# TensorE's order in the second layer: expert down products six to nine and the next group's row turning stand among other up products

## The chip, the cores and the metric

The kernel runs on one core of one Trainium2 chip. The metric is the device time of one execution in microseconds (us), as the median of several runs. In the trace the engines are called PE (TensorE, matrix products), PEld (its weight loads), DVE (VectorE), ACT (ScalarE), POOL (GpSimd) and SP (SyncE, which only issues transfers here).

## What is computed

The input is 32 sequences of 256 tokens with 128 channels. Two layers follow each other, each of the form x = x + s * g. The first has an RWKV-like branch and a small binarised feed-forward branch; the change does not touch it. The second is, cut to what matters:

```python
xn = layernorm(x)
# branch s: a selective scan
xr = xn @ W_in;  x_in, res = halves of xr
xc = silu(causal depthwise conv of 4 taps over x_in + conv_b)
p  = xc @ W_x
delta = softplus(p[:, :16] @ W_dt + b_dt);  B = p[:, 16:32];  C = p[:, 32:]
h  = h * delta + B * xc            # over time, 16 states
s  = (h.sum(states) * C * silu(res)) @ W_out
# branch g: 2 shared and 16 routed experts of width 64
shared = gelu(xn @ shared_up) @ shared_down
gate   = softmax(xn @ router), only the best 4 of 16 kept
routed = (gelu(xn @ routed_up) * gate) @ routed_down
x = x + s * silu(shared + routed)
```

## The kernel before

The 8192 tokens are cut into 16 groups (`G`) of 512. All channels lie on the 128 partitions, so one matrix product has 128 x 512 results and fills one of the eight banks of PSUM. Every engine has its own instruction list, written out by hand in program order, and the lists are tied by semaphores (`wait_ge` before an instruction, `then_inc` behind it). An engine never runs past a wait; what stands behind it in its list waits too.

The second layer is a pipeline over groups. In body n every engine works on group f = n (the front of the work: products with `W_in`, convolution, router, the experts' up products and gelus), group m = n - 1 (the scan, the experts' down products) and group t = n - 2 (the final product and sum). There are 18 bodies; in bodies 1 to 15 both f and m exist. `paired` peels the first three and the last three bodies and loops over the rest in pairs.

The experts are handled in nine pieces (`UC` = 9) of 128 rows: piece 0 holds the two shared experts, pieces 1 to 8 the routed ones. For each piece c:

- `expert_in(c)` on PE is the up product of group f: three half-precision matmuls with `upH`, `upH`, `upL` into `q_U[(c + 1) % 2]`. There are only two such banks, so for c of 2 and more it waits on `b_act` until gelu c - 2 has read its bank.
- `gelu(c)` on ACT (L613) reads that bank and writes `act[:, c, :]`.
- The gate multiplies pieces 1 to 8: POOL does pieces 1 to 3 (`GP` = 3, L443), DVE pieces 4 to 8 (`gated`, L938, which counts `b_actg`).
- `expert_out(c)` on PE is the down product of group m: one fp32 matmul with `dnT` (recorded as two passes) that adds piece c into the bank `q_F`. Its inputs were made in the body before (gelu) and by POOL or DVE.

Two more pieces of PE work stand among the up products. `turn_rows(q_D[1])` (L1069) turns the normalised rows of group f + 1 with four 128 x 128 matmuls against the identity; it waits on `b_xn` (the rows are there) and `b_cr` (DVE's `output_weight(1)`, L960, has read the bank). `gates_turned` (L1241) turns the gates of group f. ACT's `turned_high` (L537) reads the turned rows behind its gelu 5, and DVE's `turned_low` (L884) later.

Behind the last up product PE runs the final product of group m with `w_out` (it waits on `b_y`, DVE's L986), and then the next body: `low_rank` (`s1W`), `conv_in` (`w_inH`), the router, `residual_in`, `steps` (`s2W`, waits on `b_zl`, which DVE's `low_z` L943 counts), `turn_back`, `expert_out(0)` and `(1)`, `output_weights` (`wcH`, `wcL`), `s2B`, `expert_out(2)` to `(4)`, then up product 0.

ACT's list of a body, in order: `ffn_silu` (L555), `high_z` (L575), `conv_input` (L562), `step_size` (L580) and `res_silu` (L569) in turn, `conv_silu` (L588, twice), a table load (L632), exponentials and logarithms (L592, L639, L602, L596), a table load (L644), gelu 0 and 1, `high_xc(1)`, gelu 2 to 5, `turned_high`, gelu 6 to 8, `gates_out` (L550), a table load (L654).

DVE's list, in order: `row_stats` (L673), the product `sg` (L996, needs ACT's L555), `low_z` (L943, needs ACT's L575), the router's maximum (L1004, needs the router product of PE), moments, L1010, the six convolution taps (L926), the normalised rows (L891), gated pieces and `output_weight` (L960), the choice of four (L901 to L917), L1033, `scan_input` (L969), two gated pieces (L938), L953, the scans (L979), `output` (L986), `low_xc` (L965), `turned_low` (L884).

Of the kernel before, what the change touches and what calls it, by code (L numbers as in the profile page):

```python
# [39 lines left out]
def build(nc, A, out):  # L40
# [16 lines left out]
    UC = (NS + NR) * E // P  # L57
# [13 lines left out]
    with ExitStack() as ctx:  # L71
# [187 lines left out]

        b_T, b_K, b_V, b_RX, b_Z0, b_Z1, b_S, b_F = bank  # L260
        q_T, q_Q, _, _, _, _, q_S, q_F = bank
        q_D = (bank[2], bank[3])
        q_U = (bank[4], bank[5])
# [5 lines left out]
        def after(eng, semaphore, value):  # L269

            if not (isinstance(value, int) and value <= 0):
                eng.wait_ge(semaphore, value)

        def has(n):

            return not isinstance(n, int) or 0 <= n < G
# [779 lines left out]
        def _(pe):  # L1056
            def mm(ps, lhsT, rhs, start=True, stop=True):
                return nc.tensor.matmul(ps, lhsT, rhs, start=start, stop=stop)  # L1058

            def split3(ps, wh, wl, h, l):  # L1060

                mm(ps, wh, h, True, False)
                mm(ps, wh, l, False, False)
                return mm(ps, wl, h, False, True)

            def turn_rows(ps):

                for j in range(J):
                    last = nc.tensor.transpose(ps[:, j::J], xn[:, j, :], ident[:, :])  # L1069
                return last  # L1070
# [99 lines left out]
            def xc_product(ps, wh, wl, i):  # L1170
# [5 lines left out]
                    last = mm(ps[:, :], wl[:, k, w], xch[:, k, :], False, k == IC - 1)  # L1176
                return last

            def layer1(n, par):
                f, m, t = n, n - 1, n - 2  # L1180
                XH, XL = (xh, xh_)[par], (xl, xl_)[par]
# [33 lines left out]
                def expert_in(c):  # L1215
                    if c >= 2:
                        pe.wait_ge(sem["b_act"], UC * f + c - 1)
                    else:
                        pe.wait_ge(sem["b_conv"], IC * f * (TAPS - 1) + CONV_DONE[1 - c])
                    w = slice(c * P, (c + 1) * P)  # L1220
                    split3(q_U[(c + 1) % 2][:, :], upH[:, w], upL[:, w], XH[:, :], XL[:, :]).then_inc(sem["b_up"], 1)

                def expert_out(c):

                    if c > GP:
                        pe.wait_ge(sem["b_actg"], GV * m + c - GP)
                    elif c:
                        pe.wait_ge(sem["b_actp"], GP * m + c)
                    else:
                        pe.wait_ge(sem["b_act"], UC * m + 1)  # L1230
                        after(pe, sem["b_g"], m)
                    h = prod[:, c - 1, :] if c else act[:, 0, :]
                    mm(q_F[:, :], dnT[:, c * P:(c + 1) * P], h, c == 0, c == UC - 1).then_inc(sem["b_down"], 1)

                def gates_turned():
                    pe.wait_ge(sem["b_gx"], f + 1)
                    pe.wait_ge(sem["b_lg"], f + 1)
                    if has(t):
                        pe.wait_ge(sem["b_out"], t + 1)
                    for j in range(J):  # L1240
                        last = nc.tensor.transpose(q_Q[:, j::J], gx[:, j, :, :].rearrange("p r i -> p (r i)"), ident[:, :])  # L1241
                    last.then_inc(sem["b_gtT"], 1)
# [31 lines left out]
                if has(m):  # L1274
# [9 lines left out]
                    expert_out(2)  # L1284
                    expert_out(3)
                    expert_out(4)
                if has(f):
                    expert_in(0)
                    expert_in(1)
                for c in range(2, UC):  # L1290
                    if has(f):
                        expert_in(c)
                    if has(m) and c >= 5:
                        expert_out(c)
                    if has(f) and c == 5:
                        gates_turned()
                    if has(f) and has(f + 1) and c == 4:
                        pe.wait_ge(sem["b_xn"], f + 2)
                        after(pe, sem["b_cr"], IC * (m + 1))
                        turn_rows(q_D[1]).then_inc(sem["b_xnT"], 1)  # L1300
# [9 lines left out]
            pe.wait_ge(sem["prep_out"], NB)  # L1310
            pe.wait_ge(sem["prep_sbuf"], 1)
            paired(pe, layer1)


# [25 lines left out]
```

## Time and profile before

| | |
|---|---|
| time, median of 3 runs | 738.07 us (735.55 to 738.98) |
| the profiled execution's own time | 734.49 us |
| its span in the trace | 732.7 us |
| busy PE / DVE / ACT / POOL | 642.5 / 635.7 / 509.4 / 281.5 us |
| mean granted clock of TensorE | 0.976 of full |
| gelu 0 of body 1, of body 15 | at 334.54 us, at 697.31 us |

Busy time is the time in which an engine had an instruction under way; it is no proof that the engine was the limit. Times in the trace run from the span's start. The first layer and the preparation of weights fill the span up to about 300 us; the second layer fills the rest.

### The profile page before, as it was taken

What the parts mean: (1) busy time and instruction counts of PE and PEld (TensorE: products, weight loads), DVE (VectorE), ACT (ScalarE), POOL (GpSimd) and SP (SyncE); (2) the same over time, 40 slices, a digit from 0 to 9 for tenths busy, and PEclk for the clock granted to TensorE, in tenths of its full rate; (3) what the DMA queues carried; (4) which work ended last, traced back from release to release, by engine and by line L of the source; (5) the groups of instructions that cost most, each with busy time, mean ns of one, the idle gap of its engine ahead of it and who ended that gap; (6) DMA issues with size and microseconds to landing.
All of it is one profiled execution on the core that took longest, in us unless ns stands there. A gap on an engine that the chain in (4) does not pass through costs nothing. (4 is left out here: it accounts for less than half of the span.)

```text
span 732.7 us, 10841 instructions
## 1 busy us (share of the span) xinstructions
PE 642.5 (88%) x2711; PEld 304.7 (42%) x2711; DVE 635.7 (87%) x1467; ACT 509.4 (70%) x800; POOL 281.5 (38%) x278
## 2 busy tenths in 40 slices
PE   2795899999999985598999899999999999999986
PEld 1342444444444442343444444444444444544432
DVE  4996999999999997758988988988898898889766
ACT  2463566766666652687877887787788779788775
POOL 6456666777767762031222123032212303221220
PEclk9898999999999997899999999999999999999999
DMA  5420000000000000000000000000000000000000
GB/s 151 110 90 26 0 0 0 0 0 0 0 0 0 1 0 1 0 1 0 15 1 15 15 0 14 14 14 0 14 14 0 14 14 14 0 14 14 1 16 29
DMA packets 10739, 11.29 MB, mean 15 GB/s; under 512 B 4800, under 2 KB 6288, under 8 KB 10720
## 3 DMA queue, kind: packets, MB, share of 16 engines
q1 hardware_dynamic: 9744, 10.73, 4.8%
q0 software_dynamic: 112, 0.33, 0.2%
q8 instruction: 8, 0.13, 0.1%
q10 hardware_dynamic: 864, 0.00, 0.1%
q14 instruction: 11, 0.09, 0.0%
HBM read 6.87 MB, written 4.19 MB: 15 GB/s over the span
## 5 line engine op out<-in xcount | busy, mean ns | idle before, releaser
L1058 PE MATMUL bank<-arena,w 128*128 128x512 f16 x640 | 153.9, 389 | 20.0 <-DVE arena L717 14.1
L1058 PE MATMUL bank<-arena,dnT 128*128 128x512 f32 x288 | 138.6, 592 | 0.0
L613 ACT ACTIVATE arena<-bank,xinv 128x512 f32<-128x512 f32 x144 | 95.6, 687 | 51.0 <-PE bank L1058 50.8
L443 POOL TENSOR_TENSOR arena<-arena 128x512 f32<-128x512 f32 x48 | 59.7, 1271 | 151.8 <-ACT arena L550 151.8
L1058 PEld LDWEIGHTS bank<-arena,w 128*128 128x128 f16 x640 | 63.4, 100 | 99.0 <-issue 24.5
L476 ACT ACTIVATE arena<-bank 128x512 f16<-128x512 f32 x96 | 53.9, 606 | 35.1 <-PE bank L1058 35.1
L433 POOL TENSOR_TENSOR arena<-arena 128x512 f32<-128x512 f32 x16 | 17.1, 1067 | 150.5 <-DVE arena L917 150.5
L1058 PE MATMUL bank<-arena,wsqT 128*128 128x512 f32 x128 | 65.6, 617 | 6.0 <-DVE arena L726 6.0
L1058 PEld LDWEIGHTS bank<-arena,dnT 128*128 128x128 f32 x288 | 53.7, 191 | 36.0 <-issue 24.3
L926 DVE SCALAR_TENSOR_TENSOR arena<-bank,cws,arena 128x506 f32<-128x506 f32 (+1 forms) x96 | 67.1, 740 | 1.1
L717 DVE SCALAR_TENSOR_TENSOR arena<-bank,arena 128x512 f16<-128x512 f32 x96 | 60.2, 670 | 1.7 <-ACT arena L476 0.5
L938 DVE TENSOR_TENSOR arena<-arena 128x512 f32<-128x512 f32 x80 | 52.1, 684 | 0.0
L396 POOL TENSOR_TENSOR arena<-arena 128x512 f16<-128x512 f32 x32 | 36.9, 1155 | 30.3 <-ACT arena L476 22.9
L1058 PE MATMUL bank<-xh,upH 128*128 128x512 f16 x72 | 28.1, 391 | 19.4 <-ACT arena L613 15.6
L473 ACT ACTIVATE arena<-bank 128x512 f32<-128x512 f32 x32 | 19.1, 597 | 32.9 <-PE bank L1058 32.9
L996 DVE TENSOR_TENSOR sg<-bank,gp 128x512 f32<-128x512 f32 x16 | 11.1, 691 | 34.4 <-ACT gp L555 32.3
L1058 PE MATMUL bank<-xh_,upH 128*128 128x512 f16 x72 | 28.1, 390 | 14.5 <-ACT arena L613 14.5
L400 POOL TENSOR_TENSOR arena<-arena 128x512 f32<-128x512 f32 x16 | 20.3, 1269 | 51.0 <-DVE arena L753 51.0
L979 DVE TENSOR_TENSOR_SCAN arena<-arena 128x256 f32<-128x256 f32 x64 | 38.9, 669 | 0.0
L1058 PE MATMUL bank<-arena,wcH 128*128 128x512 f16 x128 | 38.1, 379 | 0.0
L1058 PEld LDWEIGHTS bank<-arena,wsqT 128*128 128x128 f32 x128 | 25.4, 200 | 22.9 <-issue 9.6
L1058 PE MATMUL bank<-arena,w_out 128*128 128x512 f32 x64 | 30.2, 594 | 3.1 <-DVE arena L986 3.1
(208 smaller groups left out, 1525.3 us busy)
## 6 DMA issues: line engine op xcount, KB each, us to landing
x_all<-in_L_attn_x SPq DMA_DIRECT2D x16, 256.0 KB, 2.7
out<-x_all SPq DMA_DIRECT2D x16, 256.0 KB, 2.0
up_n<-in_L_ffn_routed_up SPq DMA_DIRECT2D x1, 512.0 KB, 3.8
dn_n<-in_L_ffn_routed_down SPq DMA_DIRECT2D x1, 512.0 KB, 5.4
wx<-in_L_attn_W_x SPq DMA_DIRECT2D x1, 288.0 KB, 2.8
k_u<-in_L_ffn_k POOLq DMA_DIRECT2D x1, 256.0 KB, 5.1
w_in<-in_L_attn_W_in SPq DMA_DIRECT2D x1, 256.0 KB, 2.4
k_u<-in_L_ffn_k SPq DMA_DIRECT2D x1, 128.0 KB, 5.7
```

The lines of the kernel that those rows point to most:

```text
L396: g.tensor_tensor(hl[:, 1, j, :], relu[:, j, :], hh[:, 1, j, :], ALU.subtract).then_inc(sem["a_low"], 1)
L400: g.tensor_tensor(ya[:, :], ysr[:, :], rec[:, :], ALU.mult).then_inc(sem["a_y"], 1)
L433: g.tensor_tensor(gx[:, :, :, :], gt[:, :, :].unsqueeze(3).to_broadcast(wide), rs[:, :].unsqueeze(2).unsqueeze(3).to_broadcast(wide), ALU. ...
L443: g.tensor_tensor(prod[:, c, :], act[:, c + 1, :], gate[:, :], ALU.mult).then_inc(sem["b_actp"], 1)
L473: a.activation(relu[:, j, :], src, ACT.Relu).then_inc(sem["a_relu"], 1)
L476: a.activation(hh[:, layer, j, :], src, ACT.Relu).then_inc(sem[("a_hi0", "a_hi1")[layer]], 1)
L613: a.activation(act[:, c, :], q_U[(c + 1) % 2][:, :], ACT.Gelu, scale=xinv[:, I_UP:I_UP + 1]).then_inc(sem["b_act"], 1)
L717: v.scalar_tensor_tensor(hl[:, layer, j, :], b_Z[layer][j][:, :], 0.0, hh[:, layer, j, :], ALU.max, ALU.subtract).then_inc(sem[("a_lo0", " ...
L926: v.scalar_tensor_tensor(uk, seqs(q_U[k][:, :])[:, :, 0:T - back], cws[:, k, t:t + 1], uk, ALU.mult, ALU.add)\
L938: v.tensor_tensor(prod[:, c, :], act[:, c + 1, :], gate[:, :], ALU.mult).then_inc(sem["b_actg"], 1)
L979: last = v.tensor_tensor_scan(H[:, k, w], delta[:, k, w], bx[:, k, w], 0.0, ALU.mult, ALU.add)
L1058: return nc.tensor.matmul(ps, lhsT, rhs, start=start, stop=stop)
```

## The change

The table `DOWN_BEHIND` says behind which up product of group f a down product of group m stands. Before, down product c (5 to 8) stood behind up product c, and the row turning behind up product 4. After, down products 5, 6, 7 and 8 stand behind up products 1, 3, 6 and 7, and the row turning stands behind up product 1, after down product 5. `gates_turned` stays behind up product 5. Waits and increments of each moved piece go with it unchanged; nothing is added or removed.

```diff
+            DOWN_BEHIND = {1: 5, 3: 6, 6: 7, 7: 8}
+
...
-                if has(f):
-                    expert_in(0)
-                    expert_in(1)
-                for c in range(2, UC):
+                for c in range(UC):
                     if has(f):
                         expert_in(c)
-                    if has(m) and c >= 5:
-                        expert_out(c)
+                    if has(m) and c in DOWN_BEHIND:
+                        expert_out(DOWN_BEHIND[c])
                     if has(f) and c == 5:
                         gates_turned()
-                    if has(f) and has(f + 1) and c == 4:
+                    if has(f) and has(f + 1) and c == 1:
                         pe.wait_ge(sem["b_xn"], f + 2)
                         after(pe, sem["b_cr"], IC * (m + 1))
                         turn_rows(q_D[1]).then_inc(sem["b_xnT"], 1)
```

The lists of ACT, DVE and POOL stay as they are. PE's list in body 2 of the kernel before, from the last matmul of up product 1 to the row turning (`upH` and `upL` are up products of three matmuls each, `dnT` a down product, `ident,xn` the row turning):

```order
L1058 MATMUL bank<-xh,upL 128x512
L1058 MATMUL bank<-xh,upH 128x512
L1058 MATMUL bank<-xl,upH 128x512
L1058 MATMUL bank<-xh,upL 128x512
L1058 MATMUL bank<-xh,upH 128x512
L1058 MATMUL bank<-xl,upH 128x512
L1058 MATMUL bank<-xh,upL 128x512
```

The same place in the changed kernel, from the last matmul of up product 1 to down product 6:

```order
L1058 MATMUL bank<-xh,upL 128x512
L1058 MATMUL bank<-arena,dnT 128x512
L1069 MATMUL bank<-ident,xn 128x128 x4
L1058 MATMUL bank<-xh,upH 128x512
L1058 MATMUL bank<-xl,upH 128x512
L1058 MATMUL bank<-xh,upL 128x512
L1058 MATMUL bank<-xh,upH 128x512
L1058 MATMUL bank<-xl,upH 128x512
L1058 MATMUL bank<-xh,upL 128x512
L1058 MATMUL bank<-arena,dnT 128x512
```

One down product and the row turning now stand between up products 1 and 2, and another down product between 3 and 4, where up products followed each other directly.

The end of the same body on PE before, from up product 7 to the final product (`w_out`):

```order
L1058 MATMUL bank<-xh,upH 128x512
L1058 MATMUL bank<-xl,upH 128x512
L1058 MATMUL bank<-xh,upL 128x512
L1058 MATMUL bank<-arena,dnT 128x512
L1058 MATMUL bank<-xh,upH 128x512
L1058 MATMUL bank<-xl,upH 128x512
L1058 MATMUL bank<-xh,upL 128x512
L1058 MATMUL bank<-arena,dnT 128x512
L1058 MATMUL bank<-arena,w_out 128x512 x2
```

And in the changed kernel:

```order
L1058 MATMUL bank<-xh,upH 128x512
L1058 MATMUL bank<-xl,upH 128x512
L1058 MATMUL bank<-xh,upL 128x512
L1058 MATMUL bank<-arena,dnT 128x512
L1058 MATMUL bank<-xh,upH 128x512
L1058 MATMUL bank<-xl,upH 128x512
L1058 MATMUL bank<-xh,upL 128x512
L1058 MATMUL bank<-arena,w_out 128x512 x2
```

The last up product is now directly followed by the final product; no down product stands between them.

## Rows read from the trace of the kernel before

**Rows 1.** Stretch; busy PE, PEld, DVE, ACT, POOL (instructions); granted clock; DMA share; GB/s.
```profile
335.00:340.00 5.00, 4.72 (x16) 2.17 (x17) 5.00 (x9) 3.47 (x6) 0.83 (x1) 0.66 0.00 0
350.00:700.00 350.00, 325.14 (x1407) 155.09 (x1406) 312.05 (x826) 283.56 (x424) 78.96 (x80) 1.00 0.03 11
```

**Rows 2.** Who waited for whom, 350 to 720 us: total us, times, longest.
```profile
ACT arena L613 <- PE bank L1058: 45.0, 69, 1.3
...
DVE sg L996 <- ACT gp L555: 28.7, 14, 3.3
PE bank L1058 <- ACT arena L613: 24.9, 28, 1.6
```

**Rows 3.** PE in order of time, one body: start, us, what, [idle before <-releaser].
```profile
541.47 0.38 PE L1058 MATMUL bank<-xh_,upL 128*128 128x512 f16 x1
543.34 0.39 PE L1058 MATMUL bank<-xh_,upH 128*128 128x512 f16 x1 [1.50 <-ACT arena L613]
...
545.10 0.39 PE L1058 MATMUL bank<-xh_,upH 128*128 128x512 f16 x1 [0.30 <-ACT arena L613]
...
545.76 0.60 PE L1069 MATMUL bank<-ident,xn 128*128 128x128 f32 x4
...
546.85 1.02 PE L1058 MATMUL bank<-arena,dnT 128*128 128x512 f32 x2
...
552.66 1.88 PE L1058 MATMUL bank<-arena,w_out 128*128 128x512 f32 x4
554.38 1.03 PE L1058 MATMUL bank<-arena,s1W 128*128 128x512 f16 x4
...
557.58 0.59 PE L1058 MATMUL bank<-arena,s2W 128*128 128x512 f16 x2
```

**Rows 4.** ACT in order of time, the same body and the start of the next.
```profile
542.60 1.27 ACT L613 ACTIVATE arena<-bank,xinv 128x512 f32<-128x512 f32 x2
...
552.08 0.69 ACT L613 ACTIVATE arena<-bank,xinv 128x512 f32<-128x512 f32 x1 [0.82 <-PE bank L1058]
...
555.44 0.60 ACT L575 ACTIVATE arena<-bank 128x512 f16<-128x512 f32 x1 [0.28 <-PE bank L1058]
...
562.14 0.63 ACT L588 ACTIVATE arena<-arena 128x512 f32<-128x512 f32 x1 [0.81 <-DVE arena L926]
...
568.44 1.26 ACT L613 ACTIVATE arena<-bank,xinv 128x512 f32<-128x512 f32 x2
```

**Rows 5.** DVE in order of time, the same stretch.
```profile
549.36 1.26 DVE L986 TENSOR_TENSOR arena<-arena 128x512 f32<-128x512 f32 x2
...
551.87 0.68 DVE L884 SCALAR_TENSOR_TENSOR xl<-bank,xh 128x512 f16<-128x512 f32 x1
...
555.20 0.69 DVE L996 TENSOR_TENSOR sg<-bank,gp 128x512 f32<-128x512 f32 x1 [1.87 <-ACT gp L555]
556.07 0.68 DVE L943 SCALAR_TENSOR_TENSOR arena<-bank,arena 32x512 f16<-32x512 f32 x1 [0.18 <-ACT arena L575]
557.18 0.23 DVE L1004 TENSOR_REDUCE arena<-bank 128x4 f32<-128x64 f32 x1 [0.43 <-PE bank L1058]
...
557.84 4.26 DVE L926 SCALAR_TENSOR_TENSOR arena<-bank,cws,arena 128x506 f32<-128x506 f32 x6
...
566.18 0.74 DVE L960 SCALAR_TENSOR_TENSOR arena<-bank,fac,arena 128x512 f32<-128x512 f32 x1
```

**Rows 6.** ACT, gelu 0 of body 1, gelus 0 and 8 of body 15.
```profile
334.54 1.27 ACT L613 ACTIVATE arena<-bank,xinv 128x512 f32<-128x512 f32 x2
...
697.31 1.26 ACT L613 ACTIVATE arena<-bank,xinv 128x512 f32<-128x512 f32 x2
...
706.28 0.69 ACT L613 ACTIVATE arena<-bank,xinv 128x512 f32<-128x512 f32 x1 [0.82 <-PE bank L1058]
```

**Rows 7.** PE in body 0: up product 2, and the row turning.
```profile
312.23 0.61 PE L1058 MATMUL bank<-xh,upH 128*128 128x512 f16 x1 [2.93 <-ACT arena L613]
...
315.49 0.60 PE L1069 MATMUL bank<-ident,xn 128*128 128x128 f32 x4
```

## The prediction

> **What bounds the kernel now.** I read the stretches first, then the waits, then one body in order of time on PE, ACT and DVE. Between 350 and 700 us PE is busy for 325.14 of 350 us, DVE for 312.05 and ACT for 283.56 [rows 1]. No engine is full, so the period of a body is set by a loop over several engines. The waits name it: in 14 bodies PE waited 28 times for ACT's gelus, 24.9 us in all, ACT's gelus waited 69 times for PE, 45.0 us, and DVE's `sg` waited 14 times for ACT's L555, 28.7 us [rows 2].
>
> One period runs from gelu 0 at 542.60 to gelu 0 at 568.44, 25.84 us [rows 4]. Bodies 1 to 15 are 362.77 us apart over 14 periods [rows 6], 25.91 on average, so this period is typical. Its chain has five links. (a) Gelu 0 to gelu 8, 542.60 to 552.08: 9.48 us, in which ACT waits for PE (0.82 before gelu 8) [rows 4]. (b) Gelu 8 to `sg` on DVE at 555.20, through `gates_out`, a table load and L555: 3.12 us [rows 4, 5]. (c) `sg` to the first convolution tap at 557.84: 2.64 us, with three waits in or beside it: 0.28 of ACT's `high_z` for PE's `low_rank` [rows 4], 0.18 of DVE's `low_z` for `high_z`, and 0.43 of L1004 for PE's router product [rows 5]. (d) The taps, until they release ACT's second `conv_silu` at 562.14: 4.30 us. (e) ACT alone, to the next gelu 0: 6.30 us [rows 4]. The sum is 25.84.
>
> PE has holes. Up product 1's last matmul starts at 541.47 and up product 2 starts at 543.34, when gelu 0 has freed the bank. The three matmuls of an up product take 0.66 us from start to start (545.10 to the turning at 545.76), so one takes 0.22 and this hole is 1.65 us. Up products 2 and 3 end at 544.64 (543.34 + 2 x 0.65), and up product 4 starts at 545.10: a hole of 0.46. Together that is 2.11 us in a period; PE has work for the other 23.73 [rows 3].
>
> **Sizes of the moved pieces** [rows 3]. From the turning at 545.76 to down product 5 at 546.85 are 1.09 us; less an up product of 0.65 that leaves 0.44 for the turning (`gates_turned`, also four small matmuls, is put at 0.44 too). From 546.85 to `w_out` at 552.66 are 5.81 us: four down products, one `gates_turned`, three up products. (5.81 - 0.44 - 3 x 0.65) / 4 = 0.86 us for a down product.
>
> **The change, in the clock of this body.** Down product 5 and the turning (0.86 + 0.44 = 1.30) move into the first hole. They must not be late: DVE works in list order, and its second L960 is behind everything that they need (the gated piece, the normalised rows, the freed bank). It ends at 566.92, in this body's terms 25.84 earlier, at 541.08, before PE is there at 541.69 [rows 5]. So up product 2 still starts at 543.34. Up product 3 ends at 544.64, down product 6 fills the second hole and more, to 545.50, and from there PE is paced by nothing: from 543.34 on there are seven up products, `gates_turned` and three down products, 4.55 + 0.44 + 2.58 = 7.57, which ends at 550.91 instead of 552.66. PE's `w_out` comes 1.75 us earlier. It needs DVE's L986, done at 549.36 + 1.26 = 550.62 [rows 5]: 0.3 to spare. The following `w_inH` then stands at 550.91 + 1.72 + 0.86 = 553.49 and needs L884, done at 552.55 [rows 3, 5].
>
> Link (a): up product 8 is now last, with no down product behind it, so it starts 0.65 before 550.91, at 550.26; before, it started at 552.66 - 0.86 - 0.65 = 551.15, and gelu 8 followed 0.93 later. Gelu 8 moves from 552.08 to 551.19, **0.89 less**. Earlier gelus cover it: gelu 4 gets 0.4 later by down product 6, but the bank for up product 6 is free in time by a few hundredths.
>
> Link (b) is unchanged, `sg` at 554.31. Link (c): ACT could start `high_z` at 555.16 - 0.89 = 554.27, and PE's `low_rank`, 1.75 earlier, is done (555.44 - 1.75 = 553.69). So that 0.28 goes; `low_z` follows `sg` without its 0.18. L1004's 0.43 goes as well, since PE's router product is 1.75 earlier and DVE less than that. **0.61 to 0.7 less**, depending on how tightly DVE's instructions follow each other; I take 0.7, since rows that follow directly on DVE start some 0.05 to 0.1 before the end shown of the last (557.84 + 4.26 = 562.10 against 562.14 shows the other end of that spread). Links (d) and (e) hold no wait for PE. A period so loses 0.89 + 0.7 = **1.6 us**, to 24.24. PE's own check: its `steps` would start at 557.58 - 1.75 = 555.83, `low_z` ends about 555.6; and of the 2.11 us of holes 0.5 remain, before up product 2. Both loops close.
>
> **The sum.** 14 periods x 1.6 = 22.4. Body 15 has no turning: gelu 8 stands 8.97 after gelu 0 [rows 6], and would stand 8.59 after it, 0.4 less, and nothing in the tail needs the old order. In body 0 there are no down products, but the turning, which stood in a stretch that PE paced, moves into a wait of 2.93 us [rows 7]: 0.4. Together 23.2 us. The profiled execution took 734.49, so it would take 711.3. The median of the runs before is 738.07, 3.6 above the profiled one; 738.07 - 23.2 gives **714.9**. A difference within 0.5% (3.7 us) can't be told from none here.
>
> **Bounds of the unknown.** No row shows two pieces in the hole or the tightened hand-over of link (c). From above, PE's whole idle time is the most that can go in a period: 2.11 x 14 + 0.8 = 30.3. To that comes the clock of body 1 (below), at most 1.0: 738.07 - 31.3 = 706.8. From below, only gelu 8 moves and link (c) gives nothing: 0.89 x 14 + 0.8 = 13.3, so 724.8. I stay near the middle term since the three waits of link (c) are each in a row with PE or ACT as what ended them.
>
> **The rivals.**
>
> *Only link (a) shrinks.* What would hold link (c): DVE's list between `sg` and the taps finds another late partner, such as ACT's `conv_input` behind `high_z`, or PE's `w_out`, with only 0.3 to spare, waits for L986 and takes the rest of PE with it. Against it: a PE 0.3 later still has 0.5 of hole left. 724.8 us; chance 0.1.
>
> *More than forecast.* From 335 to 340 us, body 1, the granted clock is 0.66, so PE was for part of it at its lower level of 1.2 GHz instead of 2.4, behind the longest hole of that body; from 350 to 700 it is 1.00 [rows 1]. The 14 periods hold 362.77 - 14 x 25.84 = 1.0 us beyond the typical period [rows 6], the most that this lower clock can have cost. With the hole filled by 1.30 us of work the clock may stay up. Then 713.9, and with PE's holes gone too the 706.8 above; chance 0.05 for something below 711. The Trainium skill (TensorE: Matmul & The Clock Gate, "A second HAM failure mode: psum-queue depth-cycling") says that PE's short idle times between groups of matmuls can make the clock swing between its levels. By that rule every body's clock would gain from filled holes; the trace does not agree: with 2.11 us of holes in each period the clock is 1.00 over 350 us.
>
> *Slower.* The moved pieces carry their waits in front of up product 2. If the turning had to wait for DVE (`b_cr`, L960), up product 2 and all gelus would be queued behind it. Now L960 is done at 541.08, while PE is free for the turning at 542.55 and needs it done by 543.34, thus started by 542.90. The period gets longer than now only where L960 comes more than 541.08 -> 542.90 + 1.6, 3.4 us later against gelu 0. Against it: L960 and gelu 0 both follow the taps, through DVE and ACT, so nothing pulls them apart. With 4 us late in each of 14 periods it would be 0.6 x 14 = 8 us slower, 746; chance 0.03. The Trainium skill (same page, "Step-by-step: what each phase is for") states that only weight loads are pulled ahead and matmuls keep program order, which is why one late wait here would hold the ups; no run here shows it yet.
>
> *The change does nothing.* If the period were set by a loop that PE's order doesn't touch, filled holes would only reappear elsewhere. DVE is the candidate: but it idles 1.87 + 0.18 + 0.43 = 2.48 us a period, for ACT and PE [rows 5]. 738; chance 0.04.
>
> **How the numbers follow.** Forecast 0.78, only link (a) 0.1, more 0.05, none 0.04, slower 0.03. The forecast's own range is 711 to 719 (1.35 to 1.8 us a period, and the spread of the runs); with link (a) alone and the clock taken in, 709 to 723 leaves out no more than 2 in 10. Faster by over 0.5%: 0.78 + 0.1 + 0.05 = 0.93; same 0.04; slower 0.03.
>
> **What the profile after would show.** The hole before up product 2 at about 0.5 and none before up product 4; gelu 0 to gelu 8 in 8.6 us; DVE's waits before L943 and L1004 gone and the one before `sg` near 1 us; gelu 0 to gelu 0 in 24.2 us; body 1 to body 15 in 340. The prediction is wrong if `w_out` or `steps` shows a wait for DVE, or if the turning shows one for L960.

## The result

The changed kernel takes 713.89 us (median of 4 runs, 711.37 to 714.81); the kernel before took 738.04 in the same comparison (735.55 to 738.98). The ratio is 0.9694, with a 95% interval of 0.9668 to 0.972, so the gain is between 20.7 and 24.5 us. The forecast was 714.9 us, a gain of 23.2.

In the stretches (busy time of PE, PEld, DVE, ACT, POOL with instruction counts, then the granted clock), the changed kernel's PE is busy for 341.87 of 350 us, against 325.14 before [rows 1]. The first stretch lies ahead of body 1 and is taken up further down:

```profile
300.00:305.00 5.00, 4.22 (x23) 1.67 (x22) 2.33 (x14) 1.55 (x2) 0.05 (x1) 0.52 0.00 0
340.00:690.00 350.00, 341.87 (x1483) 164.34 (x1481) 326.67 (x853) 292.57 (x443) 84.35 (x84) 1.00 0.03 11
```

The waits of the changed kernel from 340 to 700 us (total us, times, longest) answer to [rows 2]. PE waits for gelus 14 times instead of 28 and for 7.5 us instead of 24.9; one of its two holes (stretches in which it idles) in each body is gone.

```profile
DVE sg L996 <- ACT gp L555: 17.8, 15, 2.8
...
PE bank L1058 <- ACT arena L613: 7.5, 14, 0.7
```

One body of the changed kernel on PE, to be held against [rows 3]:

```profile
530.61 0.38 PE L1058 MATMUL bank<-xh_,upL 128*128 128x512 f16 x1
530.83 1.02 PE L1058 MATMUL bank<-arena,dnT 128*128 128x512 f32 x2
531.69 0.60 PE L1069 MATMUL bank<-ident,xn 128*128 128x128 f32 x4
532.84 0.39 PE L1058 MATMUL bank<-xh_,upH 128*128 128x512 f16 x1 [0.56 <-ACT arena L613]
...
534.15 1.02 PE L1058 MATMUL bank<-arena,dnT 128*128 128x512 f32 x2
535.01 0.38 PE L1058 MATMUL bank<-xh_,upH 128*128 128x512 f16 x1
...
540.40 1.88 PE L1058 MATMUL bank<-arena,w_out 128*128 128x512 f32 x4
...
545.32 0.59 PE L1058 MATMUL bank<-arena,s2W 128*128 128x512 f16 x2
```

Down product 5 and the turning start without a wait right behind up product 1, down product 6 leads to up product 4 without one, and `w_out` and `steps` (`s2W`) wait for nothing; the L986 that `w_out` needs ends at 540.14, 0.26 ahead of it. The same body on ACT:

```profile
532.10 1.26 ACT L613 ACTIVATE arena<-bank,xinv 128x512 f32<-128x512 f32 x2
...
540.68 0.69 ACT L613 ACTIVATE arena<-bank,xinv 128x512 f32<-128x512 f32 x1 [0.82 <-PE bank L1058]
...
543.66 0.59 ACT L575 ACTIVATE arena<-bank 128x512 f16<-128x512 f32 x1
...
550.19 0.63 ACT L588 ACTIVATE arena<-arena 128x512 f32<-128x512 f32 x1 [0.81 <-DVE arena L926]
...
556.48 1.27 ACT L613 ACTIVATE arena<-bank,xinv 128x512 f32<-128x512 f32 x2
```

And on DVE:

```profile
538.87 1.27 DVE L986 TENSOR_TENSOR arena<-arena 128x512 f32<-128x512 f32 x2
...
543.79 0.69 DVE L996 TENSOR_TENSOR sg<-bank,gp 128x512 f32<-128x512 f32 x1 [0.95 <-ACT gp L555]
544.52 0.68 DVE L943 SCALAR_TENSOR_TENSOR arena<-bank,arena 32x512 f16<-32x512 f32 x1
545.23 0.23 DVE L1004 TENSOR_REDUCE arena<-bank 128x4 f32<-128x64 f32 x1
...
545.89 4.26 DVE L926 SCALAR_TENSOR_TENSOR arena<-bank,cws,arena 128x506 f32<-128x506 f32 x6
```

`high_z` (L575), `low_z` (L943) and L1004 had waits of 0.28, 0.18 and 0.43 before [rows 4, 5] and have none now. The period shown is 24.38; over the 12 periods from body 2 to body 14 it is 24.42 on average (the table loads L644 before gelu 0 stand at 359.86 and 652.91), against 25.85 before. The periods alternate between 24.38 or 24.39 and 24.46 or 24.47, because gelu 8 to `sg` takes 3.11 in one body and 3.20 in the next (565.06 to 568.26):

```profile
565.06 0.69 ACT L613 ACTIVATE arena<-bank,xinv 128x512 f32<-128x512 f32 x1 [0.82 <-PE bank L1058]
...
568.26 0.69 DVE L996 TENSOR_TENSOR sg<-bank,gp 128x512 f32<-128x512 f32 x1 [1.03 <-ACT gp L555]
```

The kernel before has the same 0.09 between its bodies, but there the wait for PE's router product took it up, and from body 4 to body 14 its periods lie between 25.83 and 25.85.

### The profile page after: what moved, and what is told of

Same layout as the page of the kernel before. It is cut to its first block and busy times, and to the rows that moved or that the text cites. A ratio compares the mean times of both kernels' runs of the same rounds, so it can differ in the third digit from the quotient of the medians.

```text
span 713.0 us, 10841 instructions
## 1 busy us (share of the span) xinstructions
PE 643.3 (90%) x2711; PEld 306.4 (43%) x2711; DVE 636.2 (89%) x1467; ACT 504.4 (71%) x800; POOL 281.5 (39%) x278
## 5 line engine op out<-in xcount | busy, mean ns | idle before, releaser
L588 ACT ACTIVATE arena<-arena 128x512 f32<-128x512 f32 x32 | 20.2, 631 | 20.3 <-DVE arena L926 20.3
```

Of the source, the lines that this page charges most:

```text
L588: a.activation(xc[:, par, k, :], u[:, k, :], ACT.Silu).then_inc(sem["b_xc"], 1)
```

## The experiments

The theory under test is that of the prediction, here called the loop theory: a period is gelu 0 to gelu 8, paced by the PE work between up products 2 and 8, plus the hand-over from `sg` to the taps, in which PE's `low_rank` and router product end waits only while they are late. The main rival is that PE's filled holes are all that counts. The edits below change two things in the changed kernel: the table (written with tuples, so that several down products can stand behind one up product) and the place of the turning. Times of different comparisons are set against each other by their ratios to the kernel before.

**Down product 5 alone in the hole**

```diff
-            DOWN_BEHIND = {1: 5, 3: 6, 6: 7, 7: 8}
+            DOWN_BEHIND = {1: (5,), 6: (6,), 7: (7,), 8: (8,)}
...
-                    if has(f) and has(f + 1) and c == 1:
+                    if has(f) and has(f + 1) and c == 4:
```

> The order of before, except that down product 5 stands behind up product 1 (6, 7 and 8 behind their own up products, the turning behind up product 4). Loop theory (the period is gelu 0 to gelu 8 paced by PE, plus the hand-over from sg to the taps): 0.86 us of PE work leaves the stretch between up products 2 and 8, the hole before up product 4 stays, PE and ACT both come 0.86 earlier, so high_z still waits 0.28 for PE and the hand-over gives nothing. A period 0.86 shorter, 14 x 0.86 + 0.9 = 12.9 us, about 725. Rival A (the gain comes from the end of the body, where no down product stands behind the last up product): nothing, 738. Rival B (the turning, which frees ACT's turned_high early, carries the gain): nothing, 738.

Measured: 723.12 us, ratio 0.9839 (0.9798 to 0.988); period 24.99. `high_z` still waits for PE, as this row of ACT shows:

```profile
522.68 0.60 ACT L575 ACTIVATE arena<-bank 128x512 f16<-128x512 f32 x1 [0.27 <-PE bank L1058]
```

The period is 0.86 shorter, one down product, as expected. The ratio is a gain of 1.6%, 11.7 us of 734.78, where 12.9 was expected. Both rivals gave this kernel nothing; neither can be the only source of the gain.

**The turning alone**

```diff
-            DOWN_BEHIND = {1: 5, 3: 6, 6: 7, 7: 8}
+            DOWN_BEHIND = {5: (5,), 6: (6,), 7: (7,), 8: (8,)}
```

> The order of before, except that the row turning stands behind up product 1. Loop theory: 0.44 us leaves the paced stretch, 14 x 0.44 + 0.4 = 6.6 us less, about 731.5. Rival A: nothing, 738. Rival B: most of the measured gain, about 715 to 720.

Measured: 728.82 us, ratio 0.991 (0.9876 to 0.9945); period 25.41, 0.44 shorter, as expected. The turning alone is less than a third of the 1.43 us that the change takes out of a period, so rival B falls.

**Both of them**

```diff
-            DOWN_BEHIND = {1: 5, 3: 6, 6: 7, 7: 8}
+            DOWN_BEHIND = {1: (5,), 6: (6,), 7: (7,), 8: (8,)}
```

> Both of these moves, down products 6, 7 and 8 as before. Loop theory: the two add up, 1.30 us a period, the hole before up product 4 stays at 0.46, high_z still waits 0.28 for PE: 14 x 1.30 + 1.3 = 19.5 us less, about 718.5. Rival A: 738, all of the change's gain is missing. If the two don't add up, both pieces compete for one hole of which less than 1.30 counts.

Measured: 717.6 us, ratio 0.9767 (0.9724 to 0.9809); period 24.55, 1.30 shorter. The two add up, and rival A, which gave this kernel nothing, falls. So the other moves of the change (6 behind 3, 7 behind 6, 8 behind 7) are worth only 24.55 - 24.42 = 0.13 us a period together. The next run takes them apart.

**Down product 8 behind the last up product again**

```diff
-            DOWN_BEHIND = {1: 5, 3: 6, 6: 7, 7: 8}
+            DOWN_BEHIND = {1: (5,), 3: (6,), 6: (7,), 8: (8,)}
```

> The changed kernel, except that down product 8 stands behind up product 8 again instead of behind up product 7. PE does the same work in the same holes. Loop theory: gelu 8 comes 0.86 earlier than in the changed kernel (7.7 us after gelu 0 instead of 8.6), so that PE's router product and low_rank end the hand-over again; both are 1.76 earlier than in the kernel before, so a period is 24.08 instead of 24.4: 14 x 0.33 = 4.6 us faster than the changed kernel, about 709.5. Rival C (PE alone sets the pace, and the filled holes are all that counts): as the changed kernel, 714. Rival A: slower than the changed kernel by up to 12 us, 720 to 726.

Measured: 708.37 us, ratio 0.9647 (0.9607 to 0.9687); period 24.08, as worked out. The interval of the ratio overlaps that of the changed kernel (0.9668 to 0.972); it is the periods of the traces, from body 2 to 14 24.07 or 24.08 in all but one case here and 24.38 to 24.47 there, that tell the two apart. On ACT, gelus 7 and 8 start at 533.41 and follow each other, `high_z` waits for PE once more, and the next gelu 0 is at 550.42; PE's `w_out` is at 534.64:

```profile
526.34 1.27 ACT L613 ACTIVATE arena<-bank,xinv 128x512 f32<-128x512 f32 x2
...
533.41 1.33 ACT L613 ACTIVATE arena<-bank,xinv 128x512 f32<-128x512 f32 x2 [0.82 <-PE bank L1058]
...
537.42 0.60 ACT L575 ACTIVATE arena<-bank 128x512 f16<-128x512 f32 x1 [0.27 <-PE bank L1058]
...
550.42 1.27 ACT L613 ACTIVATE arena<-bank,xinv 128x512 f32<-128x512 f32 x2
```

```profile
534.64 1.88 PE L1058 MATMUL bank<-arena,w_out 128*128 128x512 f32 x4
```

PE does the same work in the same holes as in the changed kernel, `w_out` stands 8.30 us after gelu 0 in both (540.40 - 532.10 and 534.64 - 526.34), and yet a period is 0.34 shorter. The rival that only filled holes count falls: it gives these two the same time. In the changed kernel PE had become earlier than ACT and DVE could use. Down product 6 behind up product 3 and 7 behind 6 are worth 24.55 - 24.08 = 0.47 a period, and 8 behind 7 costs 0.34 of it.

**Down products 7 and 8 behind the last up product**

```diff
-            DOWN_BEHIND = {1: 5, 3: 6, 6: 7, 7: 8}
+            DOWN_BEHIND = {1: (5,), 3: (6,), 8: (7, 8)}
```

> The changed kernel, except that down products 7 and 8 both stand behind up product 8. Loop theory, with the hand-over bound by PE as in e4 (there gelu 0 followed w_out by 15.78 us): gelu 8 comes another 0.4 earlier, at 7.3 us, but up product 8 must wait 0.4 for gelu 6 and w_out slips to 8.7 us after gelu 0. Period 8.7 + 15.8 = 24.5, as the changed kernel's 24.4 or 0.1 worse: 714 to 716 on the scale of 738 for before, ratio 0.970 to 0.973. Rival D (the sooner gelu 8, the better): another 0.4 less than e4, ratio 0.957.

Measured: 714.25 us, ratio 0.9716 (0.9675 to 0.9756); period 24.46, where 24.5 was worked out. PE's up product 8 waits for gelu 6, and `w_out` comes 515.14 - 506.46 = 8.68 us after gelu 0; ACT's `high_z` then waits 1.13 us for PE:

```profile
512.77 0.39 PE L1058 MATMUL bank<-xh,upH 128*128 128x512 f16 x1 [0.21 <-ACT arena L613]
...
515.14 1.88 PE L1058 MATMUL bank<-arena,w_out 128*128 128x512 f32 x4
```

```profile
506.46 1.27 ACT L613 ACTIVATE arena<-bank,xinv 128x512 f32<-128x512 f32 x2
...
513.71 0.69 ACT L613 ACTIVATE arena<-bank,xinv 128x512 f32<-128x512 f32 x1 [0.34 <-PE bank L1058]
...
517.92 0.60 ACT L575 ACTIVATE arena<-bank 128x512 f16<-128x512 f32 x1 [1.13 <-PE bank L1058]
```

In this kernel as in the last one the next gelu 0 follows `w_out` by 15.78 us (550.42 - 534.64, and 515.14 + 15.78 = 530.92, where the trace has it), and the kernel before has the same 15.78 (568.44 - 552.66) [rows 3, 4]. Gelu 8 stands 513.71 - 506.46 = 7.25 us after gelu 0, sooner than in any other kernel here, and the period is still longer than in the last one: rival D falls. A sooner gelu 8 is worth nothing once PE is the later partner of the hand-over.

**A down product whose input is late in the hole: the rival that ended slower**

```diff
-            DOWN_BEHIND = {1: 5, 3: 6, 6: 7, 7: 8}
+            DOWN_BEHIND = {1: (7,), 3: (5,), 6: (6,), 7: (8,)}
```

> The changed kernel with the down products permuted so that number 7 stands behind up product 1 (then 5 behind 3, 6 behind 6, 8 behind 7). Its input is DVE's third piece from the end, done 2.65 us after gelu 0, so PE must wait in front of the turning and of up product 2. This is the rival that ended slower: up product 2 starts 2.70 + 0.86 + 0.44 = 4.0 us after gelu 0 instead of 0.74, gelu 8 at 11.8, period 11.8 + 15.8 = 27.6, 1.8 more than before: 14 x 1.8 + 2 = 27 us slower than before, ratio 1.037. If TensorE's clock falls in the hole of over 3 us, up to 1.7 us more in each body, ratio up to 1.07. If matmuls could pass the waiting one, nothing of this and about 0.97.

Measured: 801.65 us, ratio 1.0887 (1.0839 to 1.0934); period 30.69. PE in one body, whose gelu 0 is at 546.84, the gated pieces 7 and 8 on DVE, and the stretches behind the hole:

```profile
549.58 2.07 PE L1058 MATMUL bank<-arena,dnT 128*128 128x512 f32 x2 [3.81 <-DVE arena L938]
551.45 1.06 PE L1069 MATMUL bank<-ident,xn 128*128 128x128 f32 x4
552.30 0.63 PE L1058 MATMUL bank<-xh,upH 128*128 128x512 f16 x1
...
554.86 1.35 PE L1058 MATMUL bank<-arena,dnT 128*128 128x512 f32 x2
556.05 0.38 PE L1058 MATMUL bank<-xh,upH 128*128 128x512 f16 x1
```

```profile
548.85 1.28 DVE L938 TENSOR_TENSOR arena<-arena 128x512 f32<-128x512 f32 x2
```

```profile
549.00:552.00 3.00, 2.42 (x5) 1.28 (x6) 3.00 (x6) 0.00 (x0) 0.00 (x0) 0.50 0.11 42
552.00:555.00 3.00, 3.00 (x10) 1.47 (x9) 3.00 (x6) 0.69 (x1) 0.00 (x0) 0.50 0.00 0
```

The waiting matmul held everything behind it: no up product passed it, and it started 2.74 us after gelu 0, where the expectation had 2.70. So this trace agrees with what the prediction takes from the Trainium skill (TensorE: Matmul & The Clock Gate, "Step-by-step: what each phase is for"), that matmuls keep program order. (Piece 7 is DVE's last but one, the first of the two in the row above, and not the third from the end, as the expectation calls it; the time given for it holds.) In addition the granted clock was 0.50 behind the hole, its lower level of 1.2 GHz: the down product took 1.87 instead of 0.86 us, the turning 0.85 instead of 0.44, two up products 2.56 instead of 1.30, the next down product 1.19 instead of 0.86. These are 3.0 us more, and 27.6 + 3.0 = 30.6, against a measured period of 30.69. The expectation's price for the clock, at most 1.7, was too low: the lower level held for more of the body's work than was put down. The waiting down product has 2.07 or 2.08 us in each body from 2 to 15, where a down product at full clock has 1.02; in body 1 it has 1.30.

**Down products 5 and 6 in the hole**

```diff
-            DOWN_BEHIND = {1: 5, 3: 6, 6: 7, 7: 8}
+            DOWN_BEHIND = {1: (5, 6), 6: (7,), 8: (8,)}
```

> Down products 5 and 6 and the turning behind up product 1, 7 behind 6, 8 behind 8. Loop theory: 2.16 us of work for a hole of 1.65 us; up product 2 starts 1.24 us after gelu 0 instead of 0.74, the hole before up product 4 is gone, w_out could start at 7.93 us after gelu 0 but waits for DVE's L986 until 8.07. Period 8.07 + 15.78 = 23.85, 0.22 less than e4, PE idle about 0.1 us a period: ratio 0.9605, the fastest. Rival E (overfilling the hole delays the gelus by what is too much, 0.5 us): period as e4's or longer, ratio 0.965 to 0.97.

Measured: 707.38 us, ratio 0.9609 (0.9563 to 0.9654); period 24.09, not 23.85: this expectation missed, and rival E, which had a period as that of the kernel with down product 8 last, is what came. The ratio of 0.9609 lies next to the expected 0.9605 all the same, but the time can't decide here: 14 periods of 0.24 more are 3.4 us, within the interval. The intervals of the two ratios overlap, and the periods are the same within 0.01. What was overlooked is in these rows of PE and ACT (gelu 0 at 527.83):

```profile
529.07 0.38 PE L1058 MATMUL bank<-xh_,upH 128*128 128x512 f16 x1
...
530.74 0.39 PE L1058 MATMUL bank<-xh_,upH 128*128 128x512 f16 x1 [0.21 <-ACT arena L613]
...
536.14 1.88 PE L1058 MATMUL bank<-arena,w_out 128*128 128x512 f32 x4
```

```profile
529.99 1.33 ACT L613 ACTIVATE arena<-bank,xinv 128x512 f32<-128x512 f32 x2 [0.29 <-PE bank L1058]
```

Up product 2 starts 1.24 us after gelu 0 as worked out, but gelu 2 moves back with it, to 2.16. Up product 4 needs gelu 2's bank, and so it has a hole in front of it again: up product 3 ends at 529.07 + 2 x 0.65 = 530.37, up product 4 starts 0.37 later. The hole before up product 4, which the expectation had as gone, is there, and `w_out` is back at 8.31.

**Both kernels once more**

> The kernel before, unchanged, to see whether TensorE's granted clock falls again in body 1 (0.66 from 335 to 340 us in the first profile, 1.00 there in the changed kernel and in e1 to e4). If the long hole before up product 2 of body 1 causes it, it is there again, and the gap from gelu 0 of body 1 to that of body 2 is 27.0 us; if it was chance, 25.9.

> The changed kernel, unchanged, to see how much of the time ahead of body 1 is chance: in its first profile gelu 0 of body 1 stood at 336.8 us, 2.3 later than in the first profile of before, with the granted clock at 0.52 from 300 to 305 us. If that is the change's doing it is there again; if it is chance, gelu 0 of body 1 comes at 333 to 336 us. The periods from body 2 on should again be 24.4 us.

Measured: 734.31 and 713.2 us, one run each. The second was run with the kernel before on one chip, which took 734.29 there, also in one run: 21.1 us apart. Clock in the kernel before, 335 to 340 us, and in the changed kernel, 300 to 305 us:

```profile
335.00:340.00 5.00, 3.37 (x17) 1.81 (x18) 4.97 (x15) 4.30 (x7) 1.04 (x1) 1.00 0.00 0
```

```profile
300.00:305.00 5.00, 3.01 (x24) 1.38 (x22) 3.73 (x13) 2.78 (x4) 1.21 (x2) 1.00 0.00 0
```

Neither low clock came back: not the 0.66 in body 1 of before [rows 1], nor the 0.52 in the changed kernel. Both are taken for chance, on one repetition each. In body 1 of before PE waits the same 2.32 us in front of up product 2 in both profiles; in the first, the matmul behind it took 0.54 and the next ones 0.63 us, in the second 0.39 and 0.38:

```profile
335.28 0.54 PE L1058 MATMUL bank<-xh_,upH 128*128 128x512 f16 x1 [2.32 <-ACT arena L613]
```

```profile
336.34 0.39 PE L1058 MATMUL bank<-xh_,upH 128*128 128x512 f16 x1 [2.32 <-ACT arena L613]
```

The table load before gelu 0 of body 1 is at 334.30 and 332.45 us, those of bodies 1 and 15 are 361.54 and 341.48 us apart, those of bodies 1 and 2 of the kernel before 25.84. The changed kernel's mean period is 24.42 again.

| kernel | period worked out | period measured | median, us | ratio |
|---|---|---|---|---|
| before | | 25.85 | 738.04 | 1 |
| the turning alone | 25.40 | 25.41 | 728.82 | 0.991 |
| down 5 alone | 24.98 | 24.99 | 723.12 | 0.9839 |
| down 5 and turning | 24.54 | 24.55 | 717.6 | 0.9767 |
| down 7 and 8 last | 24.5 | 24.46 | 714.25 | 0.9716 |
| the change | 24.24 | 24.42 | 713.89 | 0.9694 |
| down 8 last | 24.08 | 24.08 | 708.37 | 0.9647 |
| down 5 and 6 in the hole | 23.85 | 24.09 | 707.38 | 0.9609 |
| down 7 in the hole | 27.6 | 30.69 | 801.65 | 1.0887 |

Measured periods are means over bodies 2 to 14. Each ratio is against the kernel before in the same comparison, whose medians were 734.8 to 738.0.

## Why the prediction was right, and where it was off

*The holes.* Right. Down product 5 and the turning cost nothing where they stand, and everything that they need was done. The hole before up product 4 is gone. The hole left before up product 2 is 0.71 us (the turning ends at 531.69 + 0.44, up product 2 starts at 532.84), not 0.5, because the period shortened less than PE's own work moved ahead.

*Link (a).* Right to 0.01: gelu 0 to gelu 8 is 8.58 us, 0.90 less than before, and `w_out` is 1.76 earlier, where 1.75 was worked out.

*Link (b).* Unchanged, 3.11 us in the body shown and 3.20 in every second one.

*Link (c).* The mis-sized term. `sg` to the taps is 2.10 us (543.79 to 545.89) instead of 2.64: 0.54 less, where 0.7 was taken. The three waits did go, as the rows of `high_z`, `low_z` and L1004 show. But the prediction had two readings, 0.61 to 0.7, and took the larger, with the ground that DVE's instructions start a little before the last one's end; the row named for it shows an instruction of ACT that starts 0.04 after DVE's end. What was measured is below both readings. At this place DVE's instructions start after the end shown: `low_z` starts 0.73 behind `sg` and L1004 0.71 behind `low_z`, each 0.03 to 0.04 later than the end shown of a 0.69 and a 0.68 us instruction. So `sg` to `low_z` gave 0.14 and `low_z` to L1004 gave 0.40.

The links can also be read as two partners of which the later one sets the period, and this the sum of the prediction doesn't say. PE's side is `w_out` plus 15.78, as in three kernels above; ACT's and DVE's side is gelu 8 plus 15.80, where nothing behind it waits for PE (556.48 - 540.68), or 15.89 in every second body. Before, these are 10.06 + 15.78 = 25.84 and 9.48 + 15.80 = 25.28 (25.37 in every second body): PE was later, and the other side had over 0.4 to spare. In the changed kernel they are 24.08 and 24.38 or 24.47: the other side is later. In the kernels with down product 5 alone, the turning alone and both, `w_out` is at 9.20, 9.62 and 8.77 us after gelu 0, and PE's side gives 24.98, 25.40 and 24.55, against the 24.99, 25.41 and 24.55 measured. With down product 7 in the hole gelu 8 is at 14.88, and the other side gives 30.77 for the body shown, as the trace has it (546.84 to 577.61).

*The sum.* From body 1 to body 15 of the repeated profiles 361.54 - 341.48 = 20.1 us went, 1.43 a period, where 22.4 was forecast. From the table load of body 15 to the last one 28.62 us became 27.92 (696.02 to 724.64, and 677.03 to 704.95), 0.7 where 0.4 was forecast. The 0.4 of body 0 can't be told: that body differs by 2.5 us between profiles of kernels that are the same there. Together these make 20.8 to 21.2, the 21.1 of the last two runs is as much, and both stand at the lower end of the interval of 20.7 to 24.5; the rest of the measured 24.15 is smaller than the spread of single runs (732.8 to 739.1 for the kernel before in all comparisons). So the closeness of 714.9 to 713.89 is largely luck: the term of link (c) was too large by 14 x 0.16 = 2.2 us, and the comparison came out some 3 us above what the traces show. The mechanism was borne out, and the period, 1.43 less where 1.6 was forecast.

*The rivals.* "Only link (a)" did not happen, but its idea that the hand-over would not follow PE all the way was a part of the truth: PE came 1.76 earlier, the period only 1.43. "More than forecast" through the clock of body 1: in the repeated profile there was nothing to win. Its bound of 1.0 us was also a little low: bodies 1 to 15 are 362.78 and 361.54 us apart in the two profiles of before, 1.2 us with and without the low clock. "Slower" is real, as the kernel with down product 7 in the hole shows; the change did not reach the point from which it decides, since the input of down product 5 was ready when PE came to it. The Trainium skill's rule (TensorE: Matmul & The Clock Gate, "A second HAM failure mode: psum-queue depth-cycling") that short idle times make the clock swing is not borne out by the waits of 1.50 us in each body of before, where the clock was 1.00 [rows 1, 3]; behind the waits of 3.8 us, in the kernel with down product 7 in the hole, the clock was at its lower level.

## What to carry to other kernels

When several engines wait for each other once per iteration, follow one period from an instruction to its next copy and give each link its owner: work moved into a hole is worth what it takes out of a link, and no more than the next partner of that link is ready to use. Here the best single move was a down product into the hole before up product 2, and the last down product did better behind the last up product than in front of it, where it delayed the gelu that the next link waits for. Before an in-order engine gets work in front of a critical instruction, check that its inputs are ready by then; putting down product 7 instead of 5 into the hole (and 5 and 6 one place later) turned a gain of 3% into a loss of 9%.

## What was not expected of the hardware

After a hole of 3.8 us TensorE was granted 0.50 of its clock from 549 to 555 us, in a kernel that is busy around it, and the down product behind the hole was as slow in each body from 2 to 15; this cost 3.0 us a period, more than the wait itself (27.6 - 25.85 = 1.8). The clock at the start of the second layer differs between runs of one kernel (0.52 and 1.00 from 300 to 305 us), and gelu 0 of body 1 stood at 336.84 us in one profile of the changed kernel and at 333.74 in the other.
